# Attention scores regrouped to 32 tokens x 4 heads over 160 keys, with a reordered first unit, an earlier block boundary and the last gate in PSUM

## Chip, cores and metric

The kernel runs on one core of one Trainium2 chip. The metric is the device time of one execution in microseconds (us). The kernel before took 915.43 us, the median of three runs.

## What is computed

x is (2, 512, 512). After a layer norm over the last axis (no scale or shift) two branches start from the same xn and are joined at the end:

```python
q, k, v = xn @ wq, xn @ wk, xn @ wv      # 32 query heads, 8 key/value heads of 128
q, k = rope(q), rope(k)
scores = (q . k) * 128**-0.5             # each token sees itself and the 127 before it
s = softmax(scores) @ v @ wo             # (2, 512, 512)
g = silu((silu(xn @ gate) * (xn @ up)) @ down)   # 4-bit weights, inner width 1792
out = x + s * g
```

The gate, up and down weights are stored as integers with zeros and scales by groups of 128 rows.

## The kernel before

The engines are programmed by hand: each has its own list of instructions, in order, and semaphores join them. Every product of fp32 data is made of three fp32r matmuls over a high and a low part of each operand (lines 36 to 38, `three_passes`): low x high, high x low, high x high. So each operand passes through ScalarE (ACT), which writes the high part, and through GpSimd (POOL) or VectorE (DVE), which writes the low part.

**Attention block.** A unit is one key/value head of one batch (16 units, two to a pass g of the loop over heads). A unit needs six projections of 512 tokens (`project`: k, four q, v; 12 matmuls of 512 columns each), rotation of k and the q (`rope`, four VectorE steps, L891, L892, L894, L896; then high on ACT L686, low on POOL L797), and the turning of v (`turn_v`, L558). It then goes through four blocks of 128 tokens, j = 0 to 3 (n counts the 64 blocks in all). In block j TensorE turns the probabilities (`turn_probs`, L577), makes the scores of the next block (`scores`), a projection for the next unit, the output projection of the block before (`project_out`), weighs v with the turned probabilities (`weigh_values`, needs pt_lo of POOL L802) and makes another projection. The scores of one block are four groups of three matmuls, one group for each head: stationary 128 tokens of one head's q, moving 256 keys (128 for j = 0), into a quarter of two PSUM banks. VectorE folds the 256 into 128 by copying the still visible part of the block before over the masked part of the own block (L905; for j = 0 it adds a causal mask, L907), takes the maximum (L909), ACT makes four exponentials (L696), VectorE inverts the sums (L913), and ACT scales (L702).

**First unit.** Before the loop, x is read and normed in two halves (L868 on VectorE), turned on TensorE (`turn_x`, L612), and split. Projections 0 to 5 of unit 0, the rotations, the first scores, projection 0 of unit 1, and the splitting of the first output weights (L499 on POOL) follow.

**FFN block.** A barrier of all engines stands between the two blocks (L380). Gate and up are made in pieces e = 0 to 3 for each of seven pairs of inner tiles; of the first pair, e = 0, 1 and 2 are made in the attention block (`ffn_product`, EARLY_PRODUCTS), e = 3 behind the barrier. POOL clears the accumulator first (L324), then splits (L315 for the middle, L188 for weights). At the end TensorE makes eight down products, one for each 128 tokens (tile t). For each, VectorE adds it to the accumulator (L334), ACT takes silu in place (L307), POOL multiplies by y (L328), VectorE adds x (L345), and SP stores it; for the last tile VectorE does the multiplication too (L341).

## Time and profile before

| | |
|---|---|
| median of the runs | 915.43 us (915.40 to 917.39) |
| the profiled execution | 917.41 us, of it 915.6 us from the first to the last instruction (the span) |
| TensorE busy | 881.3 us, 96% of the span |
| VectorE, ACT, GpSimd busy | 658.6, 449.2, 462.7 us |
| mean granted TensorE clock | 0.992 |

In a timeline each row is an instruction or a run of equal ones, with its start, its busy time, its engine, the line of the kernel, out<-in by the program's names, and in brackets the idle time ahead of it and what ended it. Matmuls overlap, so the time that one costs is the distance from its start to the next start, which is less than its own duration.

### The profile page before, as it was taken

To read this page: it belongs to the slowest core of one execution; us is meant where nothing else is said; L and a number is where in the kernel's file an instruction comes from. 1 tells how busy PE (TensorE), PEld (TensorE's weight loads), DVE (VectorE), ACT (ScalarE), POOL (GpSimd) and SP (SyncE) were. 2 spreads that over 40 slices of the span, in tenths; PEclk is the share of its full clock that TensorE was granted. 3 is DMA by queue.
4 is the path that set the end of the run, shared out by engine and by line. 5 is a ranking of instruction groups with operands and counts; after the bars stand their busy time and mean duration, and the time that the engine had idled before them with its cause. 6 is when DMAs were issued, how large, how long until landed. Compare 5 with 4: busy or idle time off the path is not lost. (4 is left out here: it accounts for less than half of the span.)

```text
span 915.6 us, 14375 instructions
## 1 busy us (share of the span) xinstructions
PE 881.3 (96%) x4384; PEld 744.1 (81%) x4384; DVE 658.6 (72%) x1069; ACT 449.2 (49%) x1240; POOL 462.7 (51%) x358
## 2 busy tenths in 40 slices
PE   4779999999999999999999999999998999999996
PEld 3668888888888888888888888888787888888885
DVE  7767778687777868777787787778665656666656
ACT  3345565655556565555656555564652213213223
POOL 3445555555565555546555554654346435435436
PEclk9989999999999999999999999999999999999998
DMA  8010111101011010101101110002224365446542
GB/s 252 3 55 24 36 39 32 35 24 46 23 34 46 23 34 26 43 23 34 46 23 34 34 34 23 23 24 80 70 70 133 102 179 162 115 135 172 130 169 92
DMA packets 84443, 61.43 MB, mean 67 GB/s; under 512 B 3648, under 2 KB 71616, under 8 KB 84416
## 3 DMA queue, kind: packets, MB, share of 16 engines
q1 hardware_dynamic: 83696, 59.98, 22.4%
q10 hardware_dynamic: 720, 1.11, 0.3%
q8 instruction: 14, 0.23, 0.1%
q14 instruction: 13, 0.11, 0.0%
HBM read 58.98 MB, written 2.10 MB: 67 GB/s over the span
## 5 line engine op out<-in xcount | busy, mean ns | idle before, releaser
L36 PE MATMUL ps<-xt_hi,w_lo 128*128 128x512 f32 x608 | 240.9, 396 | 6.4 <-POOL w_lo L188 2.3
L37 PE MATMUL ps<-xt_lo,w_hi 128*128 128x512 f32 x608 | 239.0, 393 | 0.0
L38 PE MATMUL ps<-xt_hi,w_hi 128*128 128x512 f32 x608 | 238.2, 392 | 0.0
L797 POOL TENSOR_TENSOR q_lo<-work,q_hi 128x512 fp32r<-128x512 f32 x64 | 82.8, 1294 | 174.4 <-ACT q_hi L686 174.4
L802 POOL TENSOR_TENSOR pt_lo<-kept,pt_hi 128x512 fp32r<-128x512 f32 x112 | 143.7, 1302 | 31.0 <-ACT pt_hi L707 31.0
L36 PEld LDWEIGHTS ps<-xt_hi,w_lo 128*128 128x128 f32 x608 | 115.6, 190 | 30.2 <-issue 5.9
L38 PEld LDWEIGHTS ps<-xt_hi,w_hi 128*128 128x128 f32 x608 | 115.3, 190 | 24.7
L37 PEld LDWEIGHTS ps<-xt_lo,w_hi 128*128 128x128 f32 x608 | 115.7, 190 | 21.6
L696 ACT ACTIVATE probs<-ps,neg_max 128x128 f32<-128x128 f32 x256 | 90.7, 367 | 58.4 <-DVE neg_max L909 58.4
L707 ACT ACTIVATE pt_hi<-kept 128x512 fp32r<-128x512 f32 x112 | 69.2, 633 | 68.1 <-DVE kept L919 68.1
L36 PE MATMUL ps<-wo_hi,o_lo 128*128 (+1 forms) x256 | 99.8, 390 | 0.1
L37 PE MATMUL ps<-wo_lo,o_hi 128*128 (+1 forms) x256 | 99.6, 389 | 0.0
L38 PE MATMUL ps<-wo_hi,o_hi 128*128 (+1 forms) x256 | 99.6, 389 | 0.0
L702 ACT ACTIVATE probs<-probs,inv 128x128 f32<-128x128 f32 x256 | 81.6, 390 | 17.1 <-DVE inv L913 17.1
L686 ACT ACTIVATE q_hi<-work 128x512 fp32r<-128x512 f32 x64 | 40.5, 632 | 94.0 <-DVE work L896 94.0
L188 POOL TENSOR_TENSOR w_lo<-work,w_hi 128x512 fp32r<-128x512 f32 x42 | 57.2, 1366 | 56.8 <-ACT w_hi L183 56.8
L919 DVE TENSOR_TENSOR kept<-ps,keep_sb 128x512 f32<-128x512 f32 x112 | 72.5, 683 | 17.1 <-PE ps L577 17.1
L925 DVE TENSOR_TENSOR o_lo<-ps,o_hi 128x512 fp32r<-128x512 f32 x64 | 44.3, 692 | 51.4 <-ACT o_hi L711 51.4
L315 POOL TENSOR_TENSOR mid_lo<-kept,mid_hi 128x512 fp32r<-128x512 f32 x28 | 44.5, 1590 | 65.0 <-ACT mid_hi L292 65.0
L36 PE MATMUL ps<-k_hi,q_lo 128*128 128x256 f32 (+1 forms) x256 | 76.5, 299 | 0.0
L499 POOL TENSOR_TENSOR w_lo<-work,w_hi 128x512 fp32r<-128x512 f32 x48 | 61.8, 1297 | 23.6 <-ACT w_hi L494 23.6
L38 PE MATMUL ps<-k_hi,q_hi 128*128 128x256 f32 (+1 forms) x256 | 72.2, 282 | 0.0
(79 smaller groups left out, 1723.3 us busy)
## 6 DMA issues: line engine op xcount, KB each, us to landing
work<-L_attn_wq SPq DMA_DIRECT2D x32, 256.0 KB, 2.8
work<-L_attn_wo SPq DMA_DIRECT2D x32, 256.0 KB, 2.6
work<-L_ffn_gate_w SPq DMA_DIRECT2D x14, 256.0 KB, 3.2
work<-L_ffn_gate_z SPq DMA_DIRECT2D x14, 256.0 KB, 4.3
work<-L_ffn_gate_s SPq DMA_DIRECT2D x14, 256.0 KB, 5.4
work<-L_ffn_up_w SPq DMA_DIRECT2D x14, 256.0 KB, 3.6
work<-L_ffn_up_z SPq DMA_DIRECT2D x14, 256.0 KB, 4.1
work<-L_ffn_up_s SPq DMA_DIRECT2D x14, 256.0 KB, 4.5
```

What stands on the lines that cost most here:

```text
L36: pe.matmul(out, stat[1], mov[0], start=first, stop=False)
L37: pe.matmul(out, stat[0], mov[1], start=False, stop=False)
L38: return pe.matmul(out, stat[0], mov[0], start=False, stop=last)
L188: pool.tensor_tensor(lo, self.sh.dq(at % Shared.DQ), hi.bitcast(F32), ALU.subtract).then_inc(self.sh.w_split, 1)
L315: pool.tensor_tensor(mid_lo[:, ii, cols], mid[:, e % 2, :], mid_hi[:, ii, cols].bitcast(F32), ALU.subtract).then_inc(mid_split, 1)
L499: pool.tensor_tensor(lo, raw[p % RING][:, :], hi.bitcast(F32), ALU.subtract).then_inc(w_split, 1)
L696: act.activation(probs[:, h, :], ps_score[:, h, 1, :], ACT.Exp, bias=neg_max[:, h:h + 1], accum_out=total[:, h:h + 1]).then_inc(exp_done, 1)
L702: act.activation(probs[:, h, :], probs[:, h, :], ACT.Copy, scale=inv[:, h:h + 1]).then_inc(probs_ready, 1)
L707: act.activation(pt_hi[:, w, :], kept[:, w, :], ACT.Copy).then_inc(pt_hi_done, 1)
L797: pool.tensor_tensor(lo, roped[:, (5 * b + i) % 2, :], hi.bitcast(F32), ALU.subtract).then_inc(rope_split, 1)
L802: pool.tensor_tensor(pt_lo[:, w, :], kept[:, w, :], pt_hi[:, w, :].bitcast(F32), ALU.subtract).then_inc(pt_split, 1)
L919: dve.tensor_tensor(kept[:, w, :].rearrange("p (h c) -> p h c", h=GQ), ps_pt.rearrange("p (h c) -> p h c", h=GQ), keep[:, w, :].unsqueeze( ...
```

## The change

1. **Scores.** The stationary operand is 32 tokens x 4 heads (q is kept in that order), the moving one 160 keys, the 128 before the group's last 32 and those 32. There are again four groups of three matmuls in a block, now of 160 columns in every block; k has 128 zero columns ahead of it for j = 0. All four wait for all of the unit's q. The fold is two predicated copies of 2 x 32 columns each, for even and odd groups, and two maxima of 2 x 128 columns; for j = 0 two additions of a mask lie between. ACT reads groups 1 and 2 in two halves in swapped order. The low and high parts of q and of the attention output are written through patterns of 32 elements. The attention output has one buffer in place of two.
2. **First unit.** The first projection makes its four high x high matmuls first, then those with the low weights, then those with the low x. POOL begins with the weights only when the first half of x is normed. The second half of x is centred and scaled on ACT. The last of the four rotation steps goes from VectorE to POOL (`sum_of_roped`), with the product by the cosine written to SBUF. v is drained by ACT. The second projection of unit 1 moves ahead of the loop, the splitting of the output weights moves behind the first softmax. A fifth table (256 KB) is loaded.
3. **Block boundary.** The barrier comes before gate and up e = 2, which move behind it, as does the last addition to y.
4. **End.** Silu writes to a PSUM bank, VectorE multiplies it by y from there, and POOL adds x, except for the last tile, where VectorE adds it.

```diff
-EARLY_PRODUCTS = 3
+EARLY_PRODUCTS = 2
...
-                act.activation(acc[:, t, :], acc[:, t, :], ACT.Silu).then_inc(gate_done, 1)
+                wait(act, gated, t - 3)
+                act.activation(gate_of(t), acc[:, t, :], ACT.Silu).then_inc(gate_done, 1)
...
-                pool.wait_ge(gate_done, t + 1)
-                pool.tensor_tensor(acc[:, t, :], acc[:, t, :], sh.y[:, t, :], ALU.mult).then_inc(gated, 1)
+                pool.wait_ge(gated, t + 1)
+                pool.tensor_tensor(res[:, t, :], acc[:, t, :], res[:, t, :], ALU.add).then_inc(joined, 1)
...
-                dve.tensor_tensor(res[:, t, :], acc[:, t, :], res[:, t, :], ALU.add).then_inc(joined, 1)
+            def gate(t):
+                dve.wait_ge(gate_done, t + 1)
+                dve.tensor_tensor(acc[:, t, :], gate_of(t), sh.y[:, t, :], ALU.mult).then_inc(gated, 1)
...
-            for t in range(TT - 2, TT):
-                join(t)
-def attention_block(nc, sh, fw, x, wq, wk, wv, wo, cos_in, sin_in, causal_in, keep_in, ident_in):
+                if t >= 1:
+            dve.wait_ge(res_in, 16)
+            dve.wait_ge(gated, TT)
+            dve.tensor_tensor(res[:, TT - 1, :], acc[:, TT - 1, :], res[:, TT - 1, :], ALU.add).then_inc(last_joined, 1)
...
-        q_hi = sb("q_hi", [P, 2, GQ, SEQ], F32R)
+        q_hi = sb("q_hi", [P, 2, SEQ // QG, GQ, QG], F32R)
...
+        FOLD = (0, QG)
+        folded_scores = lambda g: ps_score[:, g, FOLD[g % 2]:FOLD[g % 2] + P]
+        both_parities = [ps_score[:, e::2, FOLD[e]:FOLD[e] + P] for e in range(2)]
...
-        BEFORE, AFTER = (1, 3, 5), (2, 4, None)
...
+            return ((2, 3, 5) if first_unit(g, b) else (1, 3, 5))[j]
+        def after(g, b, j):
+            return ((None, 4, None) if first_unit(g, b) else (2, 4, None))[j]
+        def left(g, b, j):
+            return ((1, None, 4) if first_unit(g, b) else (None, 2, 4))[j]
...
-            def scores(n, unit, b, j, heads=range(GQ)):
-                wait(pe, exp_done, n * GQ)
-                w0 = windows(j)[0]
-                for h in heads:
-                    wait(pe, rope_split, unit * 5 + (h + 2))
-                    q = [t[:, b, h, j * P:(j + 1) * P] for t in (q_hi, q_lo)]
-                    k = [t[:, b, (j - 1 + w0) * P:(j + 1) * P] for t in (k_hi, k_lo)]
-                    last = three_passes(pe, ps_score[:, h, w0:2, :].rearrange("p w c -> p (w c)"), q, k, True, True)
-                    if h == GQ - 1:
-                        last.then_inc(scores_ready, 1)
+            def scores(n, unit, b, j):
+                wait(pe, exp_done, n * NG)
+                wait(pe, rope_split, unit * 5 + 5)
+                for g in range(NG):
+                    q = [t[:, b, NG * j + g, :, :].rearrange("p h c -> p (h c)") for t in (q_hi, q_lo)]
+                    k = [t[:, b, j * P + g * QG:(j + 1) * P + (g + 1) * QG] for t in (k_hi, k_lo)]
+                    last = three_passes(pe, ps_score[:, g, 0:P + QG], q, k, True, True)
+                last.then_inc(scores_ready, 1)
...
-                    if (e, kind) == (2, GATE):
-                        pe.wait_ge(sh.silu_done, 1)
-                    if (e, kind) == (2, UP):
-                        pe.wait_ge(sh.mid_done, 1)
...
+                pe.wait_ge(xt_done, 1)
+                pe.wait_ge(w_hi_done, 1)
+                for t in range(KT):
+                    pe.matmul(out, w_hi[:, K_, t, :], xt_hi[:, t, cols], start=t == 0, stop=False)
+                pe.wait_ge(w_split, 1)
+                for t in range(KT):
+                    pe.matmul(out, w_lo[:, K_, t, :], xt_hi[:, t, cols], start=False, stop=False)
+                pe.wait_ge(xt_done, GROUP)
+                for t in range(KT):
+                    last = pe.matmul(out, w_hi[:, K_, t, :], xt_lo[:, t, cols], start=False, stop=t == KT - 1)
+                last.then_inc(proj_ready, 1)
...
-            for k in range(TURN):
-                if k == 3:
+            project_first()
+            for k in range(1, TURN):
+                if k == V_:
                     turn_x(1)
                 project(0, 0, 0, k)
+            turn_v(0, 0)
             pe.wait_ge(xt_done, TT)
-            scores(0, 0, 0, 0, range(0, 2))
-            turn_v(0, 0)
+            scores(0, 0, 0, 0)
             project(0, 1, 1, 0)
-            scores(0, 0, 0, 0, range(2, GQ))
+            project(0, 1, 1, 1)
...
+                for t in range(group * GROUP, (group + 1) * GROUP):
+                    act.activation(xin[:, t, :], xin[:, t, :], ACT.Identity, scale=-1.0, bias=mv[:, t, 0:1]).then_inc(centred, 1)
...
+            centre(1)
+            hi_of_roped(0, 0, 0)
+            scale(1)
-            hi_of_roped(0, 0, 0)
             hi_of_roped(0, 0, 1)
+            hi_of_roped(0, 0, 2)
             hi_of_x(1)
-            hi_of_roped(0, 0, 2)
             hi_of_roped(0, 0, 3)
+            hi_of_roped(0, 0, 4)
+            act.wait_ge(proj_ready, V_ + 1)
+            act.activation(v_t[:, :], bank(0, V_), ACT.Copy).then_inc(proj_drained, 1)
+            hi_of_v(0, 0)
+            exps(0)
+            normalise(0)
             for p in range(6, 8):
                 weight_hi(act, 0, p)
-            hi_of_roped(0, 0, 4)
-            hi_of_v(0, 0)
+            hi_of_roped(1, 1, 0)
             for p in range(8, 10):
                 weight_hi(act, 0, p)
-            exps(0)
-            hi_of_roped(1, 1, 0)
-            normalise(0)
...
+            def sum_of_roped(i):
+                pool.wait_ge(sin_done, 2 * i + 2)
+                pool.wait_ge(proj_drained, i + 1)
+                pool.tensor_tensor(roped_first[i % 4], roped_first[i % 4], direct[:, i % 2, :], ALU.add).then_inc(rope_sum, 1)
+            pool.wait_ge(xn_done, GROUP)
+            sum_of_roped(0)
+            sum_of_roped(1)
             for i in range(5):
                 lo_of_roped(0, 0, i)
-            for p in range(WO_, NPIECE):
+                if i + 2 < 5:
+                    sum_of_roped(i + 2)
+            pool.wait_ge(turned, TT)
+            pool.memset(y[:, TT - 1, :], 0.0).then_inc(y_zeroed, 1)
+            for p in range(WO_, WO_ + 2):
                 weight_lo(pool, 0, p)
             lo_of_roped(1, 1, 0)
-            pool.wait_ge(turned, TT)
-            pool.memset(y[:, TT - 1, :], 0.0).then_inc(y_zeroed, 1)
+            for p in range(WO_ + 2, NPIECE):
+                weight_lo(pool, 0, p)
...
+                if group:
+                    return
...
+                dve.tensor_tensor(roped_first[i % 4][0:half, :], at[half:P, :], sin[half:P, :], ALU.mult).then_inc(sin_done, 1)
+                dve.tensor_tensor(roped_first[i % 4][half:P, :], at[0:half, :], sin[0:half, :], ALU.mult).then_inc(sin_done, 1)
+                wait(dve, rope_sum, i - 1)
+                dve.tensor_tensor(direct[:, i % 2, :], at, cos[:, :], ALU.mult).then_inc(proj_drained, 1)
...
-                own = ps_score[:, :, 1, :]
-                over_h = lambda m: m.unsqueeze(1).broadcast_to([P, GQ, P])
-                    dve.copy_predicated(own, over_h(causal[:, :]).bitcast(I32), ps_score[:, :, 0, :]).then_inc(folded, 1)
-                    dve.tensor_tensor(own, own, over_h(causal[:, :]), ALU.add).then_inc(folded, 1)
-                dve.tensor_reduce(neg_max[:, :], own, mybir.AxisListType.X, ALU.max, negate=True).then_inc(max_done, 1)
+                over_g = lambda m: m.unsqueeze(1).broadcast_to([P, NG // 2, QG])
+                dve.copy_predicated(ps_score[:, 0::2, 0:QG], over_g(shown[:, 0, :]).bitcast(I32),
+                                    ps_score[:, 0::2, P:P + QG]).then_inc(folded, 1)
+                dve.copy_predicated(ps_score[:, 1::2, P:P + QG], over_g(shown[:, 1, :]).bitcast(I32),
+                                    ps_score[:, 1::2, 0:QG]).then_inc(folded, 1)
+                dve.wait_ge(folded, 2 * n + 2)
+                    for e in range(2):
+                        dve.tensor_tensor(both_parities[e], both_parities[e], absent[:, e::2, :], ALU.add).then_inc(absent_done, 1)
+                    dve.wait_ge(absent_done, 2 * unit + 2)
+                for e in range(2):
+                    dve.tensor_reduce(neg_max[:, e::2], both_parities[e], mybir.AxisListType.X, ALU.max,
+                                      negate=True).then_inc(max_done, 1)
...
+            dve.wait_ge(table_in, 80)
+            rope_first(0)
             normed(1)
-            rope(0, 0, 0)
-            rope(0, 0, 1)
+            for i in range(1, 5):
+                rope_first(i)
             lo_of_x(1)
-            rope(0, 0, 2)
-            rope(0, 0, 3)
-            rope(0, 0, 4)
-            drain_v(0, 0)
             lo_of_v(0, 0)
+            fold_and_max(0, 0, 0)
+            invert(0)
             rope(1, 1, 0)
-            fold_and_max(0, 0)
-            invert(0)
...
```

GpSimd's list ahead of the loop over heads. L499 (L525 in the change) splits weights, L797 (L882) the rotated k and q, L802 (L887) the probabilities, L893 is the new sum. Before:

```order
L499 TENSOR_TENSOR w_lo<-work,w_hi 128x512 x6
L797 TENSOR_TENSOR k_lo<-work,k_hi 128x512
L797 TENSOR_TENSOR q_lo<-work,q_hi 128x512 x4
L499 TENSOR_TENSOR wo_lo<-work,wo_hi 128x512 x4
L797 TENSOR_TENSOR k_lo<-work,k_hi 128x512
L814 MEMSET y 128x512
L802 TENSOR_TENSOR pt_lo<-kept,pt_hi 128x512
```

The same place in the change:

```order
L893 TENSOR_TENSOR work<-work 128x512
L882 TENSOR_TENSOR q_lo<-work,q_hi 128x16x32
L893 TENSOR_TENSOR work<-work 128x512
L882 TENSOR_TENSOR q_lo<-work,q_hi 128x16x32 x2
L906 MEMSET y 128x512
L525 TENSOR_TENSOR wo_lo<-work,wo_hi 128x512 x2
L882 TENSOR_TENSOR k_lo<-work,k_hi 128x512
L525 TENSOR_TENSOR wo_lo<-work,wo_hi 128x512 x2
L887 TENSOR_TENSOR pt_lo<-kept,pt_hi 128x512
```

Sums stand between the low parts of q, and the low parts of the output weights stand around the k of unit 1, with the first low part of the probabilities directly behind the last of them.

VectorE's list at the end of the program. L334 (L345 in the change) adds a down product to the accumulator, L345 (L374) adds x, L341 (L349) multiplies by y. Before:

```order
L334 TENSOR_TENSOR ffn_acc<-ps,ffn_acc 128x512
L345 TENSOR_TENSOR res<-ffn_acc,res 128x512
L334 TENSOR_TENSOR ffn_acc<-ps,ffn_acc 128x512
L345 TENSOR_TENSOR res<-ffn_acc,res 128x512 x2
L341 TENSOR_TENSOR ffn_acc<-ffn_acc,y 128x512
L345 TENSOR_TENSOR res<-ffn_acc,res 128x512
```

The same place in the change:

```order
L345 TENSOR_TENSOR ffn_acc<-ps,ffn_acc 128x512
L349 TENSOR_TENSOR ffn_acc<-ps,y 128x512
L345 TENSOR_TENSOR ffn_acc<-ps,ffn_acc 128x512
L349 TENSOR_TENSOR ffn_acc<-ps,y 128x512 x2
L374 TENSOR_TENSOR res<-ffn_acc,res 128x512
```

Behind the last accumulation stand two multiplications from PSUM and one addition, where two additions, a multiplication and an addition, all from SBUF, stood.

## Rows read from the trace of the kernel before

**Rows 1.** Page, first part: busy time, share of the span, instructions.

```profile
PE 881.3 (96%) x4384; PEld 744.1 (81%) x4384; DVE 658.6 (72%) x1069; ACT 449.2 (49%) x1240; POOL 462.7 (51%) x358
```

**Rows 2.** Timeline of the start: start us, busy us, engine, line, out<-in, count.

```profile
9.54 2.87 DVE L868 TENSOR_SCALAR y<-y,mv,rstd 128x512 f32<-128x512 f32 x4
15.38 0.79 PE L36 MATMUL ps<-xt_hi,w_lo 128*128 128x512 f32 x1 [1.41 <-DVE xt_lo L874]
...
19.39 0.58 PE L36 MATMUL ps<-xt_hi,w_lo 128*128 128x512 f32 x1
...
20.85 1.92 DVE L868 TENSOR_SCALAR y<-y,mv,rstd 128x512 f32<-128x512 f32 x4
```

**Rows 3.** Timeline of the rest of the first unit, TensorE.

```profile
41.60 0.66 PE L558 MATMUL ps<-ident_sb,v_t 128*128 128x128 f32 x4 [2.72 <-DVE v_t L879]
...
51.65 1.35 PE L577 MATMUL ps<-ident_sb,probs 128*128 128x128 f32 x4 [6.03 <-ACT probs L702]
...
62.46 0.60 PE L577 MATMUL ps<-ident_sb,probs 128*128 128x128 f32 x4
```

**Rows 4.** The same stretch, VectorE and GpSimd.

```profile
47.83 0.69 DVE L907 TENSOR_TENSOR ps<-ps,causal_sb 128x512 f32<-128x512 f32 x1
...
42.93 4.99 POOL L499 TENSOR_TENSOR wo_lo<-work,wo_hi 128x512 fp32r<-128x512 f32 x4
```

**Rows 5.** TensorE's timeline at the scores of a block 0 and a block 1.

```profile
123.24 0.30 PE L36 MATMUL ps<-k_hi,q_lo 128*128 128x128 f32 x1
...
124.90 0.40 PE L37 MATMUL ps<-xt_lo,w_hi 128*128 128x512 f32 x1
...
131.84 0.36 PE L36 MATMUL ps<-k_hi,q_lo 128*128 128x256 f32 x1
...
133.58 0.40 PE L37 MATMUL ps<-xt_lo,w_hi 128*128 128x512 f32 x1
```

**Rows 6.** VectorE by line and form: count, busy us, mean ns of one.

```profile
L909 DVE TENSOR_REDUCE neg_max<-ps 128x4 f32<-128x512 f32 x64 | 44.2, 691 | 2.2
...
L913 DVE RECIPROCAL inv<-total 128x4 f32<-128x4 f32 x64 | 10.9, 171 | 29.9 <-ACT probs L696 29.9
```

**Rows 7.** Timelines of ACT, GpSimd and TensorE in one unit, near its block j = 3.

```profile
160.59 1.27 ACT L702 ACTIVATE probs<-probs,inv 128x128 f32<-128x128 f32 x4
...
160.76 1.30 POOL L797 TENSOR_TENSOR q_lo<-work,q_hi 128x512 fp32r<-128x512 f32 x1 [2.52 <-ACT q_hi L686]
...
162.33 0.60 PE L577 MATMUL ps<-ident_sb,probs 128*128 128x128 f32 x4
...
163.12 0.30 PE L36 MATMUL ps<-k_hi,q_lo 128*128 128x128 f32 x1
```

**Rows 8.** Timelines of TensorE and GpSimd around the barrier between the blocks.

```profile
690.37 0.39 PE L38 MATMUL ps<-xt_hi,w_hi 128*128 128x512 f32 x1
...
696.55 0.39 PE L38 MATMUL ps<-xt_hi,w_hi 128*128 128x512 f32 x1
698.99 0.77 PE L36 MATMUL ps<-xt_hi,w_lo 128*128 128x512 f32 x1 [2.05 <-POOL w_lo L188]
...
702.50 0.40 PE L38 MATMUL ps<-xt_hi,w_hi 128*128 128x512 f32 x1
...
691.05 3.64 POOL L324 MEMSET ffn_acc<- 128x1024 f32 x4 [10.06 <-POOLq L380]
...
697.15 1.71 POOL L188 TENSOR_TENSOR w_lo<-work,w_hi 128x512 fp32r<-128x512 f32 x1
```

**Rows 9.** Timelines of TensorE and VectorE at the end.

```profile
907.22 0.39 PE L38 MATMUL ps<-w_hi,mid_hi 128*128 128x512 f32 x1
...
906.70 1.19 DVE L345 TENSOR_TENSOR res<-ffn_acc,res 128x512 f32<-128x512 f32 x1
907.81 0.68 DVE L334 TENSOR_TENSOR ffn_acc<-ps,ffn_acc 128x512 f32<-128x512 f32 x1
...
912.47 0.69 DVE L345 TENSOR_TENSOR res<-ffn_acc,res 128x512 f32<-128x512 f32 x1
```

185 lines of the change are left out of this document (117 added, 68 removed).

## The prediction

> **What bounds the kernel.** Read the busy times first: TensorE is busy 96% of the span, no other engine over 72% [rows 1]. So two things can give time: TensorE's own work, and the places where it stands or runs at its lower clock. For the first, look at the distances between starts in the timeline, not at durations [rows 5]. For the second, go through the list of TensorE's waits in order of time. Between 62 us and 646 us there is none; they lie at the start [rows 2, 3], around the barrier [rows 8] and behind the last matmul [rows 9]. The change touches all of these. All sums are made against the span of 915.6 us.
>
> **1. Scores.** In block 0, from the first score matmul to the second one of the projection behind, is 124.90 - 123.24 = 1.66 us (128 columns); in block 1 it is 133.58 - 131.84 = 1.74 us (256 columns) [rows 5]. Halving the columns takes off 0.08 us, so something other than columns holds the twelve matmuls. With 160 columns everywhere, 48 groups of twelve come down from 1.74 us and 16 go up from 1.66 us. The ends: 160 columns cost what 256 do (48 x 0, 16 x +0.08: 1.3 us lost), or what 128 do (48 x 0.08 = 3.8 us gained). 160 is nearer 128, and the two rows look like a floor, so I take **3.4 us gained**.
> Less one distance of 0.23 us for the projection's first matmul, the score matmuls are 0.12 us apart in block 0 and 0.126 us in block 1. The Trainium skill (TensorE: Matmul & The Clock Gate, section LDWEIGHTS) gives a stationary operand of 128 columns 128 / 1.2 = 107 ns; by that rule 160 columns, 67 ns at 2.4 GHz, lie wholly under the load, and this term would be the full 3.8 us.
>
> **2. Chain from scores to probabilities.** The slack is 162.33 against the first scaled probabilities: four in 1.27 us from 160.59, the last at 161.86, 0.8 us ahead of the transpose that needs it [rows 7]. Before, fold and maximum are two operations of 0.69 us. An operation of 4 columns took 171 ns, one of 512 columns 691 ns [rows 6], about 1 ns a column: a 64-column copy 0.24 us, a 256-column maximum 0.43 us. Unwaited ones overlap by 0.09 us, so blocks 1 to 3 take about 1.2 us where they took 1.4 us, block 0 with its two additions 2.0 us. The ends are 0.17 and 0.69 us an operation; four of 0.69 would overrun the slack by 0.4 us. I take the estimates: no wait in the loop, and **0.6 us lost** once, in the last unit, whose first block already waits for its probabilities.
> All four groups now wait for all of q. The low part of the last q ends at 160.76 + 1.30 = 162.06, the scores start at 163.12 [rows 7]: 1.06 us of slack, so nothing, as long as patterns of 32 elements cost GpSimd no more than that.
>
> **3. First unit.** I walk it with the old durations to the transposes of block n = 1, at 62.46 before [rows 3]; the same matmuls stand ahead of them in both kernels.
> - GpSimd now leaves the norming of x alone. Four operations took 2.87 us beside its work and 1.92 us without [rows 2], 0.95 us less; for the small steps ahead of them I add 0.35 us, an estimate. The first product now waits for one low part of x in place of four, one VectorE operation (0.7 us) less at the end of that queue: it starts at 13.4 us, not 15.38.
> - The early matmuls run at half clock (1.2 GHz: nine distances in 4.01 us, 0.45 us each, until 19.4 us [rows 2]; at 2.4 GHz they are 0.23 us). If the clock rises at the same moment, 2.0 us of start are worth about 1.1 us.
> - The rotation of one row goes from four VectorE steps to three, 2.9 to 2.2 us, so projections 3 and 4 find their banks free. From 13.4 us, 14 of the 72 matmuls of the six projections run by 19.4 us, 58 more take 13.2 us and the second turning of x some 1.9 us: 34.6 us. The turning of v ends at about 36 us (its wait was 2.72 us [rows 3], and ACT's copy leaves 0.8).
> - GpSimd makes the sums and low parts in turn, 1.25 us each (four in 4.99 us [rows 4]): the last low q at 36.1 us. The scores run 36.1 to 37.6 us, two projections to 43.0 us.
> - Fold started at 47.83 and the transposes at 51.65 [rows 4, 3]: 3.8 us, with the longer fold 4.4 us. From 37.8 us that is 42.2 us, under the projections. **The wait of 6.03 us goes.**
> - What is late next is GpSimd. Behind the softmax it owes two output weights, the low k of unit 1, two output weights and the low probabilities: six times 1.25 us from 43.4 us, 51.0 us. TensorE reaches the weighing of v at 47.5 us and waits 3.5 us. It then goes to the transposes of n = 1 at 51.8 us.
> 62.46 - 51.8 = 10.6 us. A standstill of 2.2 us around the barrier was followed by half clock (below, 1.7 us lost), one of 2.72 us here was not, one of 6.03 us was. I count the drop: **8.9 us gained**, ends 5 us (two more GpSimd operations late, the lower clock for twice as long) and 11.5 us.
>
> **4. Barrier.** Behind it GpSimd clears the accumulator for 3.64 us and gets to the first weights at 697.15, ending 698.86; TensorE has only e = 3 to do and stands 2.2 us (from 696.55 + 0.23 = 696.78 to 698.99). From 698.99 to 702.50 it makes eight starts in 3.51 us where 8 x 0.227 = 1.8 us do: half clock, 1.7 us lost [rows 8]. Now e = 2 and 3 stand behind the barrier, 10.9 us of matmuls against GpSimd's 7.8 us. **3.9 us gained**; ends 2 us (an ACT or VectorE step late, the drop kept) and 4.2 us. The barrier itself, 691.05 less 690.60, stays: VectorE and ACT have finished their share before the last output projection ends. The last addition to y, 0.7 us on VectorE, goes behind it in front of a dequantisation with 3 us to spare.
>
> **5. End.** The last matmul ends at 907.61; VectorE's last addition ends at 913.16, 5.5 us later, because two operations for each tile, 0.68 and up to 1.19 us beside GpSimd, fall behind TensorE's 1.36 us a tile [rows 9]. L334, which reads PSUM, keeps 0.68 us; L345, with both operands in SBUF, takes 1.19 beside GpSimd and 0.69 alone. Accumulate and gate now both read PSUM: 1.3 us a tile, which keeps up. Behind the last matmul stand accumulate 0.7, silu 0.65, gate 0.7, addition 0.7 to 1.2 us: 2.75 to 3.25 us. **2.4 us gained** (ends 1.5 and 2.7).
> The Trainium skill (GPSIMD Engine Reference, section 1, Specifications) says that GpSimd shares its SBUF interfaces with VectorE and collides with VectorE instructions of two SBUF inputs. The last addition is one and runs beside GpSimd's last: by that rule this term is 2.2 us rather than 2.7.
>
> **Sum.** 3.4 - 0.6 + 8.9 + 3.9 + 2.4 = 18.0 us off the span: 897.6 us. The profiled execution was 917.41 us, and the median of the runs is 915.43 us, which I take as the base: 915.43 - 18.0 = **897.4 us**. Within 0.3% is about what a measurement can tell from no change.
>
> **Rivals.**
> - *Short moving operands are streamed twice.* 0.12 us for 128 columns is also what two passes of 53 ns and some overhead would take, while 256 columns at 0.126 us (107 ns at 2.4 GHz) are streamed once. Then 160 columns take 133 ns and overhead, 0.14 us: a stretch of 12 x 0.14 + 0.23 = 1.91 us, 48 x 0.17 + 16 x 0.25 = 12 us lost in place of 3.4 gained, 913 us. For it: the rows don't tell a floor from a second pass. Against it: every matmul here comes with a load of its own (744 us of loads [rows 1]), which is floor enough. 8%.
> - *First unit gives half.* GpSimd's queue or the clock takes back more: 5 us instead of 8.9, and 2 instead of 3.9 at the barrier: 903 us. For it: a chain of some twenty steps on three engines, walked. 17%.
> - *Patterns of 32 elements slow GpSimd.* No GpSimd row has such a pattern. Every unit's scores wait for the last low q, in 15 units of the loop. The slack is 1.06 us; the gains of 18 us are used up when that operation takes 1.3 + 1.0 + 18 / 15 = 3.5 us. At 4.2 us it is 28 us lost, about 925 us. For it: the written pattern breaks off every 32 elements. Against it: the change keeps the number of elements, and 32 in a row are many. 5%.
> - Forecast, 70%.
>
> **Numbers.** 897.4 us. The forecast's own ends (scores -1.3 to 3.8, first unit 5 to 11.5, barrier 2 to 4.2, end 1.5 to 2.7) don't all fall together: 892 to 902. With the second rival the range is 891 to 905 us, which leaves out some 15%. Faster 0.89, same 0.06, slower 0.05.
>
> **What would show it.** TensorE: score matmuls 0.11 us apart, 1.66 to 1.69 us for the stretch above; no wait of some 6 us ahead of the first transposes, but one of about 3.5 us ahead of the first weighing of v, released by GpSimd's pt_lo; first product near 13.4 us; no wait and no half clock behind the barrier; the last VectorE addition ending 3 us behind the last matmul. The forecast is wrong if the scores cost 1.8 us or more, if TensorE waits once in every unit, or if the clock stays low behind the start.

## The result, and the profile after

The changed kernel takes 901.7 us (median of 4 runs, 900.1 to 902.1) against 916.18 us for the kernel before (4 runs, 915.4 to 917.39): a ratio of 0.984, with a 95% interval of 0.982 to 0.986. The forecast was 897.4 us, in a range of 891 to 905. The profiled execution after has a span of 900.3 us, 15.3 us less than before.

The busy times of the page, the line that answers to [rows 1]: TensorE has lost 3.9 us of busy time, so 11.4 of the 15.3 us are time in which it stood still. (Time at the low clock is inside the busy time, so this line can't tell it apart.)

```profile
PE 877.4 (97%) x4384; PEld 739.1 (82%) x4384; DVE 642.8 (71%) x1221; ACT 454.7 (51%) x1249; POOL 466.6 (52%) x363
```

The waits of TensorE in the first unit, after, from its timeline (start us, busy us, engine, line, out<-in, count, [wait <-who ended it]); it answers to [rows 2, 3]:

```profile
13.48 2.07 PE L686 MATMUL ps<-xt_hi,w_hi 128*128 128x512 f32 x4 [0.69 <-ACT xt_hi L791]
...
34.92 0.66 PE L614 MATMUL ps<-ident_sb,v_t 128*128 128x128 f32 x4 [0.99 <-ACT v_t L828]
...
36.31 0.31 PE L38 MATMUL ps<-k_hi,q_lo 128*128 128x160 f32 x1 [0.74 <-POOL q_lo L882]
...
43.22 0.60 PE L631 MATMUL ps<-ident_sb,probs 128*128 128x128 f32 x4
...
51.15 0.47 PE L38 MATMUL ps<-pt_hi,v_lo 128*128 128x512 f32 x1 [3.20 <-POOL pt_lo L887]
...
51.91 0.99 PE L631 MATMUL ps<-ident_sb,probs 128*128 128x128 f32 x4
...
66.48 0.60 PE L631 MATMUL ps<-ident_sb,probs 128*128 128x128 f32 x4
```

The wait of 6.03 us ahead of the first transposes is gone; one of 3.20 us stands ahead of the first weighing of v. The transposes of block 1 come at 51.91 us instead of 62.46. Who holds the weighing of v is in GpSimd's timeline of the same kernel, four low parts of output weights around a low k:

```profile
43.51 2.54 POOL L525 TENSOR_TENSOR wo_lo<-work,wo_hi 128x512 fp32r<-128x512 f32 x2 [6.88 <-ACT wo_hi L520]
46.01 1.30 POOL L882 TENSOR_TENSOR k_lo<-work,k_hi 128x512 fp32r<-128x512 f32 x1
47.27 2.50 POOL L525 TENSOR_TENSOR wo_lo<-work,wo_hi 128x512 fp32r<-128x512 f32 x2
49.73 1.27 POOL L887 TENSOR_TENSOR pt_lo<-kept,pt_hi 128x512 fp32r<-128x512 f32 x1
```

Behind the wait the clock is at half. The windows of the same kernel (us from:to, length, then busy us and count of PE, PEld (weight loads), DVE, ACT and POOL, then PEclk, the granted clock, and share and GB/s of the DMA):

```profile
48.00:52.00 4.00, 0.85 (x4) 0.71 (x5) 3.83 (x7) 1.92 (x7) 4.00 (x4) 1.00 0.51 149
52.00:55.00 3.00, 3.00 (x17) 3.00 (x15) 1.82 (x4) 1.93 (x4) 2.31 (x3) 0.50 0.02 6
55.00:58.00 3.00, 3.00 (x9) 2.42 (x9) 1.37 (x6) 2.32 (x10) 2.92 (x3) 0.50 0.29 87
58.00:61.00 3.00, 3.00 (x13) 2.42 (x12) 1.28 (x3) 1.39 (x6) 0.00 (x0) 0.87 0.02 5
```

The scores of a block 1, which answer to the second half of [rows 5]. What counts is the distance from one start to the next:

```profile
124.24 0.32 PE L38 MATMUL ps<-k_hi,q_lo 128*128 128x160 f32 x1
124.40 0.28 PE L39 MATMUL ps<-k_lo,q_hi 128*128 128x160 f32 x1
...
125.63 0.44 PE L38 MATMUL ps<-xt_hi,w_lo 128*128 128x512 f32 x1
125.90 0.40 PE L39 MATMUL ps<-xt_lo,w_hi 128*128 128x512 f32 x1
```

The new steps of the fold and GpSimd's strided operation, from the groups by line and form (count | busy us, mean ns of one | idle before):

```profile
L1025 DVE TENSOR_REDUCE neg_max<-ps 128x2 f32<-128x256 f32 x128 | 48.3, 419 | 2.2
L1014 DVE COPY_PREDICATED ps<-shown_sb,ps 128x64 f32<-128x64 int32 x64 | 14.3, 224 | 1.9 <-issue 1.1
```
```profile
L882 POOL TENSOR_TENSOR q_lo<-work,q_hi 128x512 fp32r<-128x512 f32 x64 | 82.7, 1293 | 144.2 <-ACT q_hi L749 144.2
```

Around the barrier ([rows 8]) the only idle time of TensorE is the barrier's own. In TensorE's timeline from 662 to 693 us there is one wait:

```profile
676.65 0.47 PE L38 MATMUL ps<-xt_hi,w_lo 128*128 128x512 f32 x1 [0.48 <-PEq L392]
```

The end, TensorE and VectorE, against [rows 9]:

```profile
894.13 0.39 PE L40 MATMUL ps<-w_hi,mid_hi 128*128 128x512 f32 x1
...
894.55 0.69 DVE L345 TENSOR_TENSOR ffn_acc<-ps,ffn_acc 128x512 f32<-128x512 f32 x1
895.16 1.44 DVE L349 TENSOR_TENSOR ffn_acc<-ps,y 128x512 f32<-128x512 f32 x2
...
896.71 1.02 DVE L374 TENSOR_TENSOR res<-ffn_acc,res 128x512 f32<-128x512 f32 x1
```

**Where the 15.3 us came from.** TensorE's order of work is the same in both kernels ahead of the barrier, so the transposes of the same block are marks in both traces, and the spans between marks can be set side by side (all in us; blocks are counted from 0, so block 60 is the first of the last unit). The forecast's term for the scores stands whole beside the second span, though it counts all 64 blocks and the span has 56 of them:

```
from, to                                     before    after    gained    forecast
start, transposes of block 3                  82.58    75.08      7.50      8.9
transposes of block 3 to those of 59         558.23   556.23      2.00      3.4
of 59 to 63 (the last unit)                   32.58    32.94     -0.36     -0.6
of 63 to the start of the last matmul        233.83   229.86      3.97      3.9
start of the last matmul to the end            8.36     6.17      2.19      2.4
sum                                                              15.30     18.0
```

These five spans are the yardstick of the experiments: all but the first and the third repeat to about 0.4 us in any execution, so one trace measures a part of the change alone.

### The profile page after: what moved, and what is told of

Same layout as the page of the kernel before. It is cut to its first block and busy times, and to the rows that moved or that the text cites. A ratio compares the mean times of both kernels' runs of the same rounds, so it can differ in the third digit from the quotient of the medians.

```text
span 900.3 us, 14582 instructions
## 1 busy us (share of the span) xinstructions
PE 877.4 (97%) x4384; PEld 739.1 (82%) x4384; DVE 642.8 (71%) x1221; ACT 454.7 (51%) x1249; POOL 466.6 (52%) x363
## 5 line engine op out<-in xcount | busy, mean ns | idle before, releaser
L887 POOL TENSOR_TENSOR pt_lo<-kept,pt_hi 128x512 fp32r<-128x512 f32 x112 | 143.6, 1302 | 33.2 <-ACT pt_hi L777 32.8
L882 POOL TENSOR_TENSOR q_lo<-work,q_hi 128x512 fp32r<-128x512 f32 x64 | 82.7, 1293 | 144.2 <-ACT q_hi L749 144.2
L772 ACT ACTIVATE probs<-probs,inv 128x128 f32<-128x128 f32 x256 | 81.6, 389 | 17.3 <-DVE inv L1030 17.3
L525 POOL TENSOR_TENSOR w_lo<-work,w_hi 128x512 fp32r<-128x512 f32 x48 | 61.4, 1289 | 26.6 <-ACT w_hi L520 16.6
L38 PE MATMUL ps<-k_hi,q_lo 128*128 128x160 f32 x256 | 74.1, 290 | 0.7 <-POOL q_lo L882 0.7
L39 PE MATMUL ps<-k_lo,q_hi 128*128 128x160 f32 x256 | 70.9, 277 | 0.0
```

The source lines that it names most:

```text
L38: pe.matmul(out, stat[1], mov[0], start=first, stop=False)
L39: pe.matmul(out, stat[0], mov[1], start=False, stop=False)
L525: pool.tensor_tensor(lo, raw[p % RING][:, :], hi.bitcast(F32), ALU.subtract).then_inc(w_split, 1)
L772: act.activation(probs[:, h, :], probs[:, h, :], ACT.Copy, scale=inv[:, h:h + 1]).then_inc(probs_ready, 1)
L882: pool.tensor_tensor(lo, by_group(row_of(unit, b, i), i), hi.bitcast(F32), ALU.subtract).then_inc(rope_split, 1)
L887: pool.tensor_tensor(pt_lo[:, w, :], kept[:, w, :], pt_hi[:, w, :].bitcast(F32), ALU.subtract).then_inc(pt_split, 1)
```

## The experiments

### The barrier and the end, one at a time

The changed kernel with three early products instead of two: gate and up of e = 2 stand ahead of the barrier again:

```diff
-EARLY_PRODUCTS = 2
+EARLY_PRODUCTS = 3
...
+            ffn_product(2, GATE)
+            ffn_product(2, UP)
```

> The changed kernel with the barrier as it was: the two products for block e=2 stand ahead of the barrier again instead of behind it (48 + 48 matmuls of 512 columns, the same number in all). Theory: the part on the barrier is worth what the trace gave, the 3.9 us of the prediction's sum (4.0 read from the difference of the two traces), because there GpSimd's w_lo holds PE and the clock falls to half: 905.7 against 901.7, with the wait for w_lo and a stretch at half clock back behind the barrier. Rival: that gain came with the shorter scores and the shifted phase of the engines ahead of it, and putting the products back costs under 1 us: 902.5 or less.

Measured: 905.69 us (median of 4). In its trace the span from block 63 to the last matmul is 233.77 us against 229.86, 3.91 us more; all else is as in the changed kernel. TensorE's timeline and the windows of this kernel bring back what [rows 8] showed, the standstill for w_lo and the half clock behind it:

```profile
690.14 0.49 PE L38 MATMUL ps<-xt_hi,w_lo 128*128 128x512 f32 x1 [2.02 <-POOL w_lo L191]
```
```profile
688.00:691.00 3.00, 0.98 (x5) 0.74 (x5) 2.96 (x3) 0.89 (x2) 3.00 (x3) 0.99 0.00 0
691.00:694.00 3.00, 3.00 (x9) 2.33 (x8) 2.96 (x3) 0.74 (x3) 2.38 (x2) 0.50 0.62 171
```

So the order of the products alone is worth the 3.9 us, and the rival that is named there falls.

The changed kernel with the old end:

```diff
...
-                act.activation(gate_of(t), acc[:, t, :], ACT.Silu).then_inc(gate_done, 1)
+                act.activation(acc[:, t, :], acc[:, t, :], ACT.Silu).then_inc(gate_done, 1)
...
-                pool.tensor_tensor(res[:, t, :], acc[:, t, :], res[:, t, :], ALU.add).then_inc(joined, 1)
+                pool.tensor_tensor(acc[:, t, :], acc[:, t, :], sh.y[:, t, :], ALU.mult).then_inc(gated, 1)
...
```

> The changed kernel with the end as it was: silu is written to SBUF, GpSimd multiplies by the gate and VectorE adds the residual, two steps later. Theory: the end is worth the 2.2 us that the two traces differ by behind the last matmul (sum of the prediction 2.4): 903.9 against 901.7. Rival: the end's own rows are as they were before, but the earlier last matmul of the changed kernel already holds part of it (VectorE or GpSimd catches up behind the last product in either form): under 1 us, 902.6 or less.

Measured: 903.6 us (median of 4); last matmul to end 8.36 us, to the hundredth that of the kernel before, against 6.17. The end is worth 2.19 us.

The changed kernel with one part of that end taken out: silu goes to SBUF, the rest of the new order stays.

```diff
-        gate_of = lambda t: ps[:, t % 4, :]
+        gate_of = lambda t: acc[:, t, :]
```

> The changed kernel, with silu of the gate at the end written back to SBUF, so that VectorE's multiplication reads two SBUF operands while GpSimd adds two SBUF operands; in the changed kernel it reads one from PSUM (0.69 us each). Theory, that the two engines hinder each other there, as VectorE's 1.08 us first row of norming and GpSimd's did at the start of the kernel before: the multiplications take 1.0 to 1.5 us instead of 0.69 and the end behind the last matmul 6.9 to 7.7 us instead of 6.17. Rival: the final gate gains by its engine alone and not by PSUM: multiplications of 0.69 us, end 6.2 to 6.4 us.

Measured: 904.6 us (median of 5) against 900.04 us for the changed kernel on the same chip in the same rounds; last matmul to end 9.96 us. Both the theory (6.9 to 7.7 us) and its rival were too small. VectorE's and GpSimd's timeline of this kernel, its first multiplication and a later one:

```profile
885.15 0.68 DVE L349 TENSOR_TENSOR ffn_acc<-ffn_acc,y 128x512 f32<-128x512 f32 x1
...
893.51 0.68 DVE L345 TENSOR_TENSOR ffn_acc<-ps,ffn_acc 128x512 f32<-128x512 f32 x1
893.67 1.27 POOL L339 TENSOR_TENSOR res<-ffn_acc,res 128x512 f32<-128x512 f32 x1 [0.63 <-DVE ffn_acc L349]
...
894.12 1.37 DVE L349 TENSOR_TENSOR ffn_acc<-ffn_acc,y 128x512 f32<-128x512 f32 x1
...
895.41 0.68 DVE L345 TENSOR_TENSOR ffn_acc<-ps,ffn_acc 128x512 f32<-128x512 f32 x1
```

The gate's multiplication takes 1.37 us instead of the 0.68 that L349 takes in the changed kernel, while L345, which reads PSUM beside the same GpSimd operation, stays at 0.68. The same line at 885.15, made while GpSimd stands idle, takes 0.68 too, so two operands in SBUF are not slow by themselves. I had the price of one right (1.0 to 1.5 us) and not counted how many tiles it adds up over: accumulate and gate are now 1.9 us a tile (893.51 to 895.41 from one L345 to the next), TensorE makes one in 1.36, and VectorE falls 0.54 us further behind with each of the later tiles. Without the gate in PSUM the new order would be 1.6 us worse than the old end, not 2.2 us better. The Trainium skill (GPSIMD Engine Reference, section 1, Specifications) says that GpSimd's SBUF interfaces are shared with VectorE and collide with VectorE instructions of two SBUF inputs; these rows agree: L349, with both inputs in SBUF, overlaps GpSimd's operation and doubles; L345, with one in PSUM, overlaps it and doesn't.

### The scores

Four kernels with other numbers of columns in the score matmuls and nothing else changed. In the first three `wide` is 256, 192 and 128 in all four groups, in the fourth it is 256 in the last group only. They compute other scores than those asked for, and each ran once; what is read is the trace:

```diff
...
-                    k = [t[:, b, j * P + g * QG:(j + 1) * P + (g + 1) * QG] for t in (k_hi, k_lo)]
-                    last = three_passes(pe, ps_score[:, g, 0:P + QG], q, k, True, True)
+                    at = min(j * P + g * QG, P + SEQ - wide)
+                    k = [t[:, b, at:at + wide] for t in (k_hi, k_lo)]
+                    last = three_passes(pe, ps_score[:, g, 0:wide], q, k, True, True)
```

> The changed kernel, but each score matmul moves 256 columns of keys instead of 160 (the values are not the scores asked for, only the time is read; all else as it is). Read on the stretch from the transposes of block 3 to those of block 59, 556.2 us in the changed kernel and 558.2 in the kernel before, so that the clock in the first unit and the last plays no part. Theory: a score matmul costs its weight load (0.111 us) up to 160 columns and its columns above (0.119 at 256): 12 x 0.008 + 0.05 for the first, 0.12 us a block less what the projection's first matmuls give back, together as in the kernel before: 558.0 to 560 (3.6 at most, 56 blocks x 0.064, without give-back). Rival, that the columns alone count (0.107 at 256 if 2.4 columns a ns, 0.067 at 160): 556.2 + 56 x 12 x 0.04 = 583.

> As the one with 256 columns, with 192 (only the time is read, the scores are not those asked for). Theory, the load is the floor: 0.111 us a matmul as with 160, the stretch 556.2 to 556.6 us. Rival, by columns: 556.2 + 56 x 12 x 0.013 = 565.

> As the one with 256 columns, with 128 (the scores of the last 32 keys of each window are left out, only the time is read). Theory, the load is the floor: 0.111 us as with 160, the stretch 555.6 to 556.3 us. Rival, by columns: 556.2 - 56 x 12 x 0.013 = 547. Second rival, that short matmuls are streamed twice below some width: 547 or less, or a pitch that jumps.

> As the changed kernel, with 256 columns in the last of the four groups of score matmuls alone (3 of 12; only the time is read, the last group's scores are not those asked for). What is asked is where 0.04 to 0.07 us a block went that the projection behind the scores took longer (its first matmul 0.271 instead of 0.234 and small parts of the next). Theory: the weight loads run ahead of long matmuls and fall behind during short ones; three long ones at the group's end let them catch up: the projection's 12 matmuls take 2.75 us as in the kernel before, the three cost 0.02 more, the stretch comes out at 555.2 to 556.2 us, not above. Rival: the give-back hangs on the sum of the short ones, not on the last: the projection stays at 2.79 to 2.82, the stretch at 556.2 to 557.8.

Measured, all from the timelines, medians over blocks 4 to 59, for j = 1 to 3 (us); "group" is the twelve score matmuls, "behind" the twelve matmuls of the projection that follows, "first" its first distance:

```
columns               group          behind         first    both            blocks 3 to 59
256 (before, j>0)     1.507-1.509    2.748          0.233    4.255-4.257     558.23
256 in all            1.494-1.510    2.720-2.747    0.23     4.214-4.254     559.06
192                   1.402-1.404    2.766-2.803    0.254    4.168-4.207     555.78
160 (changed)         1.385-1.387    2.785-2.821    0.272    4.170-4.208     556.23
128                   1.371-1.373    2.782-2.799    0.284    4.154-4.170     555.15
160, last group 256   1.438-1.445    2.737-2.759    0.233    4.175-4.197     556.04
```

Within a group the eleven distances behind the first average 0.112 us at 128, 160 and 192 columns (single ones 0.107 to 0.117) and 0.119 us at 256. All that the groups of 128, 160 and 192 columns differ by lies in their first distance: 0.143, 0.157 and 0.173 us (0.203 at 256).

What follows. There is a floor of 0.112 us for these matmuls, up to 192 columns: the rivals by columns (583, 565 and 547 us for 256, 192 and 128 columns) are off by 8 us and more. The forecast's rival of two passes is dead too, by the runs with 160 and 192 columns, for which twice the columns would be 0.133 and 0.160 us; at 128 columns two passes of 53 ns would not be told from the floor. The traces also show that it is the load: at 128, 160 and 192 columns the group's weight loads (PEld) all start 0.110 to 0.112 us apart and each matmul some 0.06 to 0.09 us behind its load, while at 256 columns each load starts only when the matmul ahead of it does, 0.117 to 0.121 us apart in most cases. The Trainium skill (TensorE: Matmul & The Clock Gate, section LDWEIGHTS) gives 107 ns for a load of 128 columns; the trace has 0.112. The stretches with 192 and 128 columns came out 0.4 and 0.45 us below the bands expected for them. But part of what the group gains, the matmuls behind it give back: with 160 columns the group is 0.12 us shorter than with 256, the projection 0.037 to 0.073 us longer, some 0.04 of it in its first distance (0.272 against 0.233) and the rest in small parts of the next ones. The fourth kernel tells where that comes from, and here my expectation was half wrong. Three long score matmuls at the end do bring the projection back to 2.74 to 2.76 us, but they cost 0.05 us themselves and not 0.02 (0.157 us pass from the first of them to the second, where 0.119 is usual at 256 columns), so the sum stays (4.175 to 4.197). The price of leaving a run of short matmuls is paid once, by the first long one, whoever it belongs to.

Two things stay open. The same twelve projection matmuls take 2.785 or 2.821 us behind otherwise equal blocks, and which blocks have which differs between kernels whose TensorE program is the same (the kernels with the old end and with the gate in SBUF have 555.94 and 555.87 us in this stretch); that is 0.3 us of the 2.0, and the 192 and 160 columns can't be told apart because of it. And 256 columns in all came out at 559.06, above the 558.23 of the kernel before: its block 0 has them too and takes 4.260 us for both groups instead of 4.160, blocks 1 and 2 take 0.03 to 0.04 us less than before; over 14 units that is 0.45 us, about half of the difference.

### The start

The changed kernel, GpSimd no longer waiting for the norming of x, and the first projection in its old order:

```diff
-            project_first()
-            for k in range(1, TURN):
+            pe.wait_ge(xt_done, GROUP)
+            for k in range(TURN):
...
-            pool.wait_ge(xn_done, GROUP)
```

> The changed kernel with the start as it was: GpSimd does not wait for the norming of x, and the first projection runs in its old order of matmuls behind all parts of x. Theory: VectorE's norming of x takes 2.87 us from 9.5 again instead of 1.92 from 8.5, the transposes of x come 1.1 us later, and the rest of the start (the first projection's high products while low parts are still made) is worth another 0 to 0.7: scores of block 0 at 37.4 to 38.1 instead of 36.3, time 902.8 to 903.5 against 901.7. Rival: the chain of rotations on VectorE, not the first projection, sets the scores of block 0: they stay at 36.3 to 36.8 and the time within 0.5 us.

Measured: 901.91 us (median of 5, 900.78 to 905.53) against 900.04 for the changed kernel beside it: 1.9 us between medians, which the scatter hardly clears. The timeline of this kernel has the old start back ([rows 2]):

```profile
9.58 2.87 DVE L968 TENSOR_SCALAR y<-y,mv,rstd 128x512 f32<-128x512 f32 x4
10.27 3.65 PE L665 MATMUL ps<-ident_sb,y 128*128 128x128 f32 x16 [10.27 <-DVE y L968]
...
15.33 0.79 PE L38 MATMUL ps<-xt_hi,w_lo 128*128 128x512 f32 x1 [1.41 <-DVE xt_lo L974]
```

The scores of block 0 start at 37.65 us, 1.3 us later than the 36.31 above and inside what was expected. Of the 7.5 us of the first unit I put 1.3 to 1.9 down to the start and the rest to the chain from rotation to probabilities, which isn't measured by a run of its own. The mark at block 3 can't settle it: it is at 73.75 us here, between the 75.08 and the 71.87 us of the two traces of the changed kernel, for the reason that the next section gives.

### The backlog of GpSimd and the half clock

Three kernels ask whether the 3.2 us wait, and the half clock behind it, can be had. The first moves two low parts of output weights behind the first pt_lo (and the second all four):

```diff
-            for p in range(WO_ + 2, NPIECE):
-                weight_lo(pool, 0, p)
...
+                        if first_unit(g, b) and j == 0:
+                            for p in range(WO_ + 2, NPIECE):
+                                weight_lo(pool, 0, p)
```

> The changed kernel, with one thing moved: GpSimd makes the low parts of output weights 8 and 9 behind the first pt_lo instead of ahead of it. In the changed kernel PE stands 3.2 us at the first weighing of values (51.15), waiting for that pt_lo (49.73, 1.27), and the granted clock is then at half from 51.9 to 58.5. Theory: GpSimd's backlog is the cause of the wait and the standstill is the cause of the half clock. Two pieces of about 1.3 us leave the path, so pt_lo starts about 2.5 us sooner and the wait falls from 3.2 to about 0.9 us; the transposes of block 1 come at about 50.1 (then bounded by ScalarE's normalising) instead of 51.9, 1.8 us; and if 0.9 us is too short for the clock to fall, another 3.1 us: 4.9 us faster, 896.8 against 901.7. Rival A: the clock falls there all the same (it fell at 50.5 in the kernel before too, with another wait): only 1.8 us faster or less, 899.9. Rival B: another chain was late all along (the DVE and ScalarE rows of block 1): the wait moves to the transposes, nothing gained, 901.7.

> The changed kernel with all four low parts of output weights 6 to 9 behind the first pt_lo on GpSimd (VectorE and ScalarE as they are). In the variant that moved two of them the profiled run had no half clock behind block 1 and took 898.0, but its median was 900.5. Theory: PE still stands 0.6 us at the transposes of block 1 (ScalarE's normalising, behind the rotation), they come at 50.3 as in that variant, and what is left is chance of the clock: with the wait for pt_lo gone altogether the clock falls more rarely: median 899 to 900. Rival: the clock falls behind any short wait alike: median 900.5 or above. Second rival: the output weights' low parts are now late for the first output product (a wait of up to 2 us on o_lo or wo_lo at about 57): 901 to 902.

The third moves all four, and in the first block the inversion and normalising of block 1 ahead of the rotation of the next rows:

```diff
+                        sooner = first_unit(g, b) and j == 0
+                        if sooner:
+                            invert(n + 1)
...
-                        if more:
+                        if more and not sooner:
...
```

> The changed kernel, with all four low parts of output weights 6 to 9 behind the first pt_lo on GpSimd, and, in the first block alone, the inversion and the normalising of block 1 ahead of the rotation of the next rows on VectorE and of their high parts on ScalarE. Theory: with GpSimd's backlog gone the next thing late is the normalising of block 1 (1.26 us per four, ends 51.04), held by the rotation in front of it; with both moved the transposes of block 1 come at about 48.9 instead of 51.9: 3.0 us, and 3.1 us more if the clock does not fall to half: 6.1 us faster, 895.6. Rival A: the clock falls all the same: 3.0 us faster, 898.7. Rival B: the rows that were pushed back (rotation and high parts of the second rows of K and Q, output weights) are now late for the scores and the first output product, and the time is given back: under 1 us faster, 901 or above.

And the changed kernel itself once more, for its scatter:

> The changed kernel itself once more, beside the others of this call, for its scatter. Theory, from the first four runs with traces of variants: everything but the stretches at half clock repeats to 0.1 us (transposes of block 3 to those of block 59: 556.2; block 63 to the last matmul: 229.9; end behind it 6.2), and the runs differ by which short standstills of PE are followed by a stretch at half clock: behind the 3.2 us wait always (3 to 7 us long, 1.5 to 3.1 us lost), behind the 1.4 us wait at block 60 sometimes (1 to 1.5 us lost). Then its runs lie between 900.0 and 903.5, with lower mean clock the longer ones, median 901.7. Rival: the first four runs were a lucky draw, or the scatter has another source: runs above 904, or times that do not go with the mean clock.

Measured (us, runs in their order):

```
                                                                 median   ratio to before, 95%
changed kernel, first    902.1   901.79  901.62  900.1           901.7    0.984  (0.982 to 0.986)
changed kernel, again    899.95  900.19  899.07  900.95  900.04  900.04   0.982  (0.980 to 0.983)
two parts moved          897.98  900.52  901.95  900.3   902.17  900.52   0.984  (0.982 to 0.985)
four parts moved         899.13  901.69  900.31  902.01  899.71  900.31   0.983  (0.981 to 0.984)
four parts and softmax   903.16  901.33  902.95  899.97  901.02  901.33   0.984  (0.982 to 0.985)
```

In the profiled run of the first (897.98 us) the theory looks proved to the tenth. Its timeline and windows:

```profile
48.81 0.47 PE L38 MATMUL ps<-pt_hi,v_lo 128*128 128x512 f32 x1 [0.78 <-POOL pt_lo L887]
...
50.31 1.21 PE L631 MATMUL ps<-ident_sb,probs 128*128 128x128 f32 x4 [0.57 <-ACT probs L772]
...
62.28 0.60 PE L631 MATMUL ps<-ident_sb,probs 128*128 128x128 f32 x4
```
```profile
52.00:55.00 3.00, 3.00 (x18) 2.59 (x18) 1.82 (x4) 1.85 (x4) 2.35 (x3) 1.00 0.33 97
```

The wait falls from 3.20 to 0.78 us, block 1's transposes come 1.6 us sooner, the clock stays up and block 2's come 4.2 us sooner; the span is 4.1 us shorter. Yet the median, 900.52, gains nothing against the nine runs of the changed kernel (median 900.2). A part of the reason is in the repeat of the changed kernel. Its timeline and windows:

```profile
34.37 0.66 PE L614 MATMUL ps<-ident_sb,v_t 128*128 128x128 f32 x4 [2.38 <-ACT v_t L828]
...
35.76 0.31 PE L38 MATMUL ps<-k_hi,q_lo 128*128 128x160 f32 x1 [0.74 <-POOL q_lo L882]
...
44.27 0.60 PE L631 MATMUL ps<-ident_sb,probs 128*128 128x128 f32 x4
...
51.08 0.47 PE L38 MATMUL ps<-pt_hi,v_lo 128*128 128x512 f32 x1 [2.12 <-POOL pt_lo L887]
...
51.85 0.63 PE L631 MATMUL ps<-ident_sb,probs 128*128 128x128 f32 x4
...
63.22 0.60 PE L631 MATMUL ps<-ident_sb,probs 128*128 128x128 f32 x4
```
```profile
14.00:17.00 3.00, 3.00 (x15) 2.45 (x14) 2.97 (x10) 1.83 (x3) 1.66 (x2) 1.00 0.95 249
36.00:39.00 3.00, 3.00 (x16) 2.71 (x16) 1.51 (x6) 0.00 (x0) 0.09 (x1) 0.61 0.00 0
48.00:52.00 4.00, 1.88 (x10) 1.23 (x9) 3.80 (x8) 2.61 (x11) 3.93 (x4) 1.00 0.50 148
52.00:55.00 3.00, 3.00 (x23) 2.74 (x21) 1.78 (x3) 1.74 (x4) 1.30 (x2) 1.00 0.01 4
638.00:641.00 3.00, 3.00 (x13) 2.67 (x13) 2.40 (x7) 0.91 (x4) 1.81 (x2) 0.53 0.22 63
```

The same program has the half clock elsewhere. In the first trace the first products run at half rate (8 matmuls in the window from 14 to 17 us; four starts of L686 take 1.87 us, 0.47 each, and 1.03 us in the repeat), the wait for v_t is 0.99 us, and the clock falls at 52. PEclk reads 1.00 in this window of both traces, so the half rate of the start is read from the distances alone. In the repeat they run at full rate (15 in the same window), TensorE gets to v_t sooner and stands 2.38 us, and the clock falls at 36.7, during the scores. There it costs the transposes of block 0 about 1.6 us (8.5 us from the scores instead of 6.9), but not the weighing of v, which GpSimd's backlog holds until 51.08 in any case; and no fall comes at 52. In this trace the low clock is hidden under the backlog. Of the thirteen traces of the changed kernel and its variants, seven have the first pattern of the start and five the second; the one with the old start is a case of its own. My expectation for the repeat, a fall behind the wait for pt_lo always and runs from 900.0 to 903.5 us, missed: its wait there was 2.12 us with no fall behind it, and two of its five runs lie below 900. What the thirteen traces do show is that the clock fell behind the wait for pt_lo in all five that have it at 3.20 to 3.27 us, and in none of the five that have it at 1.69 to 2.12 us.

Why the median of the kernel without the backlog gains nothing stays argued. It gained 4 us in the first pattern; in the second it may have less to hide the low clock under. For its slower runs there is only the mean clock (1.000 in the run of 897.98 us, 0.996 in those of 900.3 and 900.5, 0.994 in the two of about 902), and none of their traces was kept. The kernel with four parts moved, 900.31 us, has no trace of the second pattern either: in the one that it has, of the first, the wait for pt_lo is 0.33 us, 1.02 us stand ahead of block 1's transposes at 50.30, the clock doesn't fall, and there is no late output weight, which its second rival had named.

A second place is the wait of 1.4 us at block 60, [1.39 <-ACT probs L772] in the changed kernel. In nine of the thirteen traces the clock falls behind it (0.53 in the last window above), in four it does not, the first trace of the changed kernel among them. From block 60 to 63 it is 25.04 to 25.09 us without a fall and 26.05 to 27.63 with one.

The third kernel shows the other side of moving work. Block 1's transposes come at 50.19 us, hardly sooner than in the first (though this trace is of the second pattern, whose low clock at 34 to 41 us is ahead of them), and now the row that was pushed back is late. TensorE's, then ScalarE's timeline of this kernel:

```profile
50.19 1.21 PE L631 MATMUL ps<-ident_sb,probs 128*128 128x128 f32 x4
57.51 0.47 PE L38 MATMUL ps<-wo_hi,o_lo 128*128 128x512 f32 x1 [1.98 <-DVE o_lo L1044]
```
```profile
55.53 0.63 ACT L749 ACTIVATE q_hi<-work 128x512 fp32r<-128x512 f32 x1 [2.27 <-DVE work L1009]
56.06 0.58 ACT L781 ACTIVATE o_hi<-ps 128x512 fp32r<-128x512 f32 x1
```

o_hi is queued on ScalarE behind the q_hi of the delayed rotation, so TensorE stands 1.98 us at the output product, and the clock falls behind that (0.50 from 58 to 61 us). This is rival B of this kernel's expectation. No kernel tried here is shown to be faster than the changed one.

## Why the prediction was right, and where its sizes were off

- **Scores** (3.4 us forecast, 3.0 of it for the 56 blocks in which 2.0 were measured). The two rows of [rows 5] were read rightly as a floor, though the 0.12 and 0.126 us a matmul are averages that take in a long first distance (0.144 and 0.203 us) and, in block 0, too little for the projection's first (0.23 for 0.286): the others are 0.112 and 0.119 us apart. That is why the rival of two passes could look open, and the stretch to the second projection matmul came out as forecast (125.90 - 124.24 = 1.66 us). The mis-sized term is what lies behind the stretch: the twelve matmuls of the projection were taken to cost the same behind short score matmuls as behind long ones. Behind 160 columns they take 0.04 to 0.07 us more than behind 256, so j = 1 and 3 gain 0.047 us a block, j = 2 0.087, and j = 0 loses 0.027. Reading [rows 5] on to the end of the projection in block 0 would have shown it, 2.789 us against 2.748.
- **Chain to the probabilities** (no wait in the loop, 0.6 us lost once). Right: the rows have 224 and 419 ns for the estimates of 0.24 and 0.43 us, no wait stands in the loop, the wait at block 60 went from 0.89 to 1.39 us, and the last unit lost 0.36. The pattern of 32 elements costs GpSimd 1293 ns, as before; that rival falls.
- **First unit** (8.9 forecast, 7.5 measured). The walk gave 51.8 us for block 1's transposes, 3.5 us of wait and 51.0 us for the end of pt_lo; the trace has 51.91, 3.20 and 51.00. That these agree is in part luck, since the start did not run as the walk had it: the walk let the half rate of the start last until 19.4 us, in this trace it ends at about 17.8 and in the repeat the products run at full rate from 13.58 on. GpSimd's backlog levels that out: block 1's transposes are at 51.91 and 51.85 us. What was off is the price of the low clock, 1.7 us taken over from the barrier. Behind a 3.2 us wait it lasted from 52 to beyond 58 us: from block 1's to block 2's transposes it is 14.57 us here and 11.37 in the repeat, 3.2 us lost. The forecast treated the fall as a fixed property of the place; it differs between executions of one program, and the repeat has gained 10.71 us at block 3 where the first trace has 7.50.
- **Barrier** (3.9 us forecast, 3.97 between the traces, 3.91 by its own run) and **end** (2.4 forecast, 2.19). Both right, and each borne out by a run of its own. By the Trainium skill's rule named in the forecast (GPSIMD Engine Reference, section 1, Specifications) the end was 2.2 us. That is what was measured: the last addition, with two operands in SBUF and GpSimd at work until 897.18, took 1.02 us (896.71). The run with the gate in SBUF shows how much hangs on it.
- **Against the measured time.** The terms miss 2.7 us (18.0 less 15.3). The other 1.6 of the 4.3 us between 897.4 and 901.7 come from the base: the sum belongs to an execution of 917.41 us and was taken off a median of 915.43. Taken off its own execution it gives 899.4, against 902.1 for the one after. The misses of the two large terms both point the same way, so the time is not right by errors that cancel; it is inside the range by the width of the range. The repeat, at 900.04, is nearer the forecast than the first four runs; I count that as scatter, not as support.
- **The two large rivals.** Two passes for short operands is ruled out by 160 and 192 columns at the same 0.112 us. "First unit gives half" named the right weak spot, GpSimd and the clock, at 8.9 - 1.4 rather than 5.

## What to carry to other kernels

Time a group of short matmuls to the end of the long ones behind it; the load floor is real, and so is the price of leaving it. Before you move a late engine's work to shorten a standstill of TensorE, ask what the standstill hides, and judge by the median: in one execution the wait hid 1.6 us that an earlier stretch of low clock had cost, and taking the wait away made one run 4 us shorter and the median no shorter. Where VectorE's steps end the kernel, put one operand of each into PSUM while GpSimd works in SBUF, and count the steps per tile against TensorE's time per tile.
